# A graph attention stage: 8 of 25 lifts per head made by ScalarE and GpSimd, the rows of maxima read from PSUM by VectorE, and a new order on ScalarE

## The reference, cut to what matters

```python
h = (x @ W).reshape(N, H, C)
al_s = jnp.einsum('nhc,hc->nh', h, a_src)
al_d = jnp.einsum('nhc,hc->nh', h, a_dst)
e = jax.nn.leaky_relu(al_s[src] + al_d[dst], 0.2)
m = jax.ops.segment_max(e, dst, num_segments=N)
ex = jnp.exp(e - m[dst])
denom = jax.ops.segment_sum(ex, dst, num_segments=N)
out = jax.ops.segment_sum(h[src] * (ex / denom[dst])[:, :, None], dst, num_segments=N)
```

## Time and profile before

| | |
|---|---|
| median of the three runs | 4491.51 us |
| the profiled execution's own time | 4485.12 us |
| its span | 4483.3 us |
| VectorE (DVE) busy over the span | 2860.0 us, 64% |
| TensorE (PE) busy | 3600.2 us, 80% |
| ScalarE (ACT) busy | 2241.0 us, 50% |
| GpSimd (POOL) busy | 708.7 us, 16% |
| mean granted TensorE clock | 0.882 of full speed |

### The profile page before, as it was taken

The page is one execution under the profiler, slowest core; times in us unless marked ns, Lnnn a source line. Parts: engine busy times, 40 slices in busy tenths (PEclk is TensorE's granted clock), DMA queues, the critical chain, the costliest instruction groups (busy, mean ns, idle before and its releaser), DMA issues. The chain is left out here.

```text
span 4483.3 us, 70197 instructions
## 1 busy us (share of the span) xinstructions
PE 3600.2 (80%) x21308; PEld 2884.0 (64%) x21309; DVE 2860.0 (64%) x6577; ACT 2241.0 (50%) x5503; POOL 708.7 (16%) x491
## 2 busy tenths in 40 slices
PE   4766999989869999836999999899899268886391
PEld 3333555568768999825777777777778257775160
DVE  6877887811141000239999999999997529996312
ACT  4981367820033444325666666666665457763030
POOL 2991000000023000400111111111110000000404
PEclk9557999999969999958999999999999689996595
DMA  4970234554231111231111111111100323321223
GB/s 121 221 174 13 88 146 177 232 220 147 99 110 45 55 55 55 74 142 35 44 43 43 43 43 43 43 43 43 38 32 39 134 92 107 106 91 39 78 76 107
DMA packets 100401, 396.61 MB, mean 88 GB/s; under 512 B 11870, under 2 KB 56386, under 8 KB 77266
## 3 DMA queue, kind: packets, MB, share of 16 engines
q1 hardware_dynamic: 82940, 344.48, 22.3%
q0 software_dynamic: 14976, 44.58, 3.2%
q10 hardware_dynamic: 2368, 6.03, 0.6%
HBM read 270.45 MB, written 124.59 MB: 88 GB/s over the span
## 5 line engine op out<-in xcount | busy, mean ns | idle before, releaser
L1298 PE MATMUL gat_agg<-f_XN,gat_A 128*128 128x257 f32 x5000 | 1132.8, 385 | 22.1 <-DVE gat_A L1403 22.1
L1298 PEld LDWEIGHTS gat_agg<-f_XN,gat_A 128*128 128x128 f32 x5000 | 956.0, 193 | 163.2 <-DVE gat_A L1403 22.7
L1232 ACT ACTIVATE kept_X<-kept_X,gat_s 128x128 f32<-128x128 f32 x2500 | 741.4, 387 | 481.5 <-DVE kept_X L1392 481.5
L1392 DVE SCALAR_TENSOR_TENSOR kept_X<-gat_r,gat_s 128x128 f32<-128x128 f32 x2500 | 664.9, 345 | 45.8 <-POOL gat_r L1180 45.7
L2312 ACT ACTIVATE moe_exp_h<-moe_exp_hbank,moe_b1c 128x128 f32<-128x128 f32 x742 | 271.3, 367 | 541.1 <-PE moe_exp_hbank L2263 364.8
L868 PE MATMUL mat_cw<-mat_join,mat_lane 128*128 128x400 f16 x2976 | 509.8, 334 | 35.1 <-issue 19.2
L868 PEld LDWEIGHTS mat_cw<-mat_join,mat_lane 128*128 128x128 f16 x2976 | 290.7, 98 | 254.7 <-issue 48.1
L1365 DVE CUSTOM_DVE_ANT_0 gat_junk<-gat_als,gat_absT 128x3200 bf16<-128x3200 f32 x100 | 348.1, 3481 | 25.4 <-DMA gat_als<-score_rows 16.5
L2270 PE MATMUL moe_exp_ybank<-moe_exp_w2b,moe_exp_h 128*128 128x256 f32 x1484 | 350.0, 384 | 9.5 <-DVE kept_X L2332 3.4
L1403 DVE SCALAR_TENSOR_TENSOR gat_A<-kept_X,gat_C 128x1664 f32<-128x1664 f32 x200 | 354.1, 1812 | 0.0
L2346 DVE TENSOR_TENSOR moe_exp_xgT<-moe_exp_ybank,moe_b 128x256 f32 x109 | 46.3, 425 | 460.0 <-PE moe_exp_ybank L2270 460.0
(11 more groups left out here) (369 smaller groups left out, 4699.7 us busy)
## 6 DMA issues: line engine op xcount, KB each, us to landing
gat_C<-count_matrix SPq DMA_DIRECT2D x50, 1600.0 KB, 6.5
count_matrix<-mat_both SPq DMA_DIRECT2D x25, 1600.0 KB, 5.3
weight_matrix<-mat_both SPq DMA_DIRECT2D x25, 1600.0 KB, 8.8
edge_raw<-in_edge_attr_dram SPq DMA_DIRECT2D x50, 768.0 KB, 6.1
e_WT<-weight_matrix SPq DMA_DIRECT2D x13, 1600.0 KB, 6.6
sum_more<-weight_matrix SPq DMA_DIRECT2D x12, 1600.0 KB, 6.6
slot_rows<-moe_exp_xgT POOLq DMA_DIRECT2D x22, 640.0 KB, 3.7
hidden<-gat_h1t SPq DMA_DIRECT2D x25, 512.0 KB, 2.8
```

Of the source, the lines that this page charges most:

```text
L1232: last = nc.scalar.activation(w, w, ACT.Exp, bias=s02[:, t, h:h + 1])
L1298: last = nc.tensor.matmul(agg[h % 2][:, 0:D + 1], A[h % 2][:, t, :], g.XN[:, t, :], start=(t == 0), stop=(t == NT - 1))
L1392: last = nc.vector.scalar_tensor_tensor(out=work[h % 2][:, t * P:(t + 1) * P], in0=r1[:, h, :], scalar=s08[:, t, h:h + 1], in1=r2[:, h, :] ...
```

## The change

In both functions:

- The lift of the last 8 of the 25 tiles of sources (`POOL_TILES`) leaves VectorE. It is written as r2 + max(0.8 d + 0.8 s, 0), which equals max(r1 + s08, r2) since r1 - r2 = 0.8 d. ScalarE makes the positive part (`raise_low`, 8 activations of 128 x 128 into the new buffer `low`), which needs no maximum; GpSimd adds r2 in one instruction of 128 x 1024 (`share`) into `work`. The second half of exps waits for it.
- `rows` moves from GpSimd to VectorE, two instructions per tile, and reads the maxima straight from the PSUM bank. `keep_max` and `m_row` go. `m_diag` goes as well: spread_max multiplies the column m, read as a matrix with equal columns, by the identity (four products of 128 columns in `gat_heads`).
- `low` has one buffer: raise_low of a head waits for the share of the head before it.

In `gat_heads` alone: ScalarE does raise_low of the head after next, then ends, then exps (before: exps, then ends); invert comes before lift; spread_max(i+1) moves to the middle of head 1, behind turn_absent(i+2); rows(i+1) stands in VectorE's list of head 3, ahead of top; the load of `ar` has its own semaphore and waits for raise_low. In `gat_single` alone: rows(i+2) stands between add_output(i-2) and weigh(i), and the bias is added to X at the start, after self_loops(1), not at the end.

```diff
@@ gat_heads: GpSimd
-            def rows(i):
...
+            def share(i, h):
+                n = i * UN + h
+                if h == 0:
+                    wait_alone(pool, r_ready, i * 2 + 2)
+                if not (starts(i) and h < 2):
+                    wait_alone(pool, A_ready, n * 2 - 2)
+                wait_alone(pool, low_ready, n + 1)
+                nc.gpsimd.tensor_tensor(work[h % 2][:, (NT - POOL_TILES) * P:NT * P].rearrange("p (t d) -> p t d", d=P),
+                                        low[:, :].rearrange("p (t d) -> p t d", d=P),
+                                        r2[:, h, :].rearrange("p (o d) -> p o d", o=1).to_broadcast([P, POOL_TILES, P]),
+                                        ALU.add).then_inc(share_ready, 1)
@@ gat_heads: ScalarE
             def exps(i, h):
                 for part, half in enumerate(halves):
                     act.wait_ge(u_ready, (i * UN + h) * 2 + part + 1)
+                    if part == 1:
+                        act.wait_ge(share_ready, i * UN + h + 1)
...
                     ni, nh = following(i, h)
+                    si, sh = following(ni, nh)
+                    if not near_end(si, 0):
+                        raise_low(si, sh)
+                    ends(i, h)
                     if not near_end(ni, 0):
                         exps(ni, nh)
-                    ends(i, h)
                     if h == 1 and not near_end(i, 2):
                         absents(i + 2)
-                    if h == 2 and not near_end(i, 1):
-                        keep_max(i + 1)
...
+            def raise_low(i, h):
+
+                if h == 0:
+                    wait_alone(act, ar_in, i * 16 + 16)
+                if not (starts(i) and h == 0):
+                    wait_alone(act, share_ready, i * UN + h)
+                for t in range(NT - POOL_TILES, NT):
+                    o = t - (NT - POOL_TILES)
+                    last = nc.scalar.activation(low[:, o * P:(o + 1) * P],
+                                                ar[:, at(i % 2), h, :].rearrange("p o d -> p (o d)"), ACT.Relu,
+                                                scale=1.0 - SLOPE1, bias=s08[:, t, h:h + 1])
+                last.then_inc(low_ready, 1)
@@ gat_heads: TensorE
+            def between(i):
+                if not near_end(i, 2):
+                    turn_absent(i + 2)
+                if not near_end(i, 1):
+                    spread_max(i + 1)
+
             def body(i):
                 first = starts(i)
                 for h in range(H1):
-                    head(i, h, first and h < 2,
-                         (lambda: turn_absent(i + 2)) if h == 1 and not near_end(i, 2) else None)
-                    if h == 1 and not near_end(i, 1):
-                        spread_max(i + 1)
+                    head(i, h, first and h < 2, (lambda: between(i)) if h == 1 else None)
@@ gat_heads: VectorE
+            def rows(i):
+
+                mine = ar[:, at(i % 2), :, :].rearrange("p o h d -> p (o h d)")
+                top_row = mrow[:, 0:H1 * P]
+                dve.wait_ge(mrow_ready, i + 1)
+                dve.wait_ge(ar_in, i * 16 + 16)
                 if not starts(i):
...
+                    dve.wait_ge(share_ready, i * UN)
+                    dve.wait_ge(u_ready, i * UN * 2)
+                nc.vector.tensor_tensor(r1[:, :, :].rearrange("p h d -> p (h d)"), mine, top_row,
+                                        ALU.subtract).then_inc(r_ready, 1)
+                nc.vector.scalar_tensor_tensor(out=r2[:, :, :].rearrange("p h d -> p (h d)"), in0=mine, scalar=SLOPE1,
+                                               in1=top_row, op0=ALU.mult, op1=ALU.subtract).then_inc(r_ready, 1)
...
                 for half in halves:
-                    for t in range(half.start, half.stop):
+                    for t in range(half.start, min(half.stop, NT - POOL_TILES)):
...
+                    if h == 3 and not near_end(i, 1):
+                        rows(i + 1)
                     if h == 3 and not near_end(i, 2):
                         top(i + 2, 0)
-                    ni, nh = following(i, h)
-                    if not near_end(ni, 0):
-                        lift(ni, nh)
                     if h >= 2:
                         invert(i, h - 2, starts(i))
                     elif not starts(i):
                         invert(i - 1, H1 + h - 2, False)
+                    ni, nh = following(i, h)
+                    if not near_end(ni, 0):
+                        lift(ni, nh)
@@ gat_single: TensorE
                 if not (isinstance(i, int) and i == 0):
-                    pe.wait_ge(mrow_kept, i)
-                nc.tensor.matmul(mrow[:, 0:P], g.ones[:, :], m_diag[:, :], start=True, stop=True).then_inc(mrow_ready, 1)
+                    pe.wait_ge(r_ready, i * 2)
+                nc.tensor.matmul(mrow[:, 0:P], m[:, 0:1].to_broadcast([P, P]), g.ident[:, :],
+                                 start=True, stop=True).then_inc(mrow_ready, 1)
@@ gat_single: VectorE
                 if not (isinstance(i, int) and i < 2):
                     add_output(i - 2, b)
+                if not near_end(i, 2):
+                    rows(i + 2, b)
                 weigh(i, b)
```

More of the change, by code:

```diff
@@ L1048, in _ @@
             sp.wait_ge(stored, n * 16)
+POOL_TILES = 8
 def gat_heads(nc, sems, g, X):
@@ L1283, in spread_max @@
                 if not starts(i):
-                    pe.wait_ge(mrow_kept, i)
-                nc.tensor.matmul(mrow[:, 0:H1 * P], g.ones[:, :], m_diag[:, :, :].rearrange("p h d -> p (h d)"),
-                                 start=True, stop=True).then_inc(mrow_ready, 1)
+                    pe.wait_ge(r_ready, i * 2)
+                for h in range(H1):
+                    last = nc.tensor.matmul(mrow[:, h * P:(h + 1) * P], m[:, h:h + 1].to_broadcast([P, P]), g.ident[:, :],
+                                            start=True, stop=True)
+                last.then_inc(mrow_ready, 1)
             def head(i, h, early, middle=None):
@@ L1449, in _ @@
             dve.wait_ge(x_out, 16)
+            rows(0)
             lift(0, 0)
@@ L1728, in exps @@
                     act.wait_ge(u_ready, i * 2 + (part + 1))
+                    if part == 1:
+                        act.wait_ge(share_ready, i + 1)
                     for t in range(half.start, half.stop):
@@ L1734, in body, with raise_low @@
             def body(i, b):
+                if not near_end(i, 2):
+                    raise_low(i + 2)
                 if not near_end(i, 1):
                     exps(i + 1, 1 - b)
-                if not near_end(i, 2):
-                    keep_max(i + 2)
                 if not near_end(i, 4):
                     absents(i + 4)
+            def raise_low(i):
+                wait_alone(act, c_in, i * 32 + 32)
+                if not (isinstance(i, int) and i == 0):
+                    wait_alone(act, share_ready, i)
+                for t in range(NT - POOL_TILES, NT):
+                    o = t - (NT - POOL_TILES)
+                    last = nc.scalar.activation(low[:, o * P:(o + 1) * P], ar[:, slot(i), :].rearrange("p o d -> p (o d)"),
+                                                ACT.Relu, scale=1.0 - SLOPE1, bias=s08[:, t:t + 1])
+                last.then_inc(low_ready, 1)
             absents(0)
             absents(1)
-            keep_max(0)
+            act.wait_ge(scaled_s, 1)
+            raise_low(0)
             absents(2)
-            keep_max(1)
             absents(3)
-            act.wait_ge(scaled_s, 1)
             exps(0, 0)
+            raise_low(1)
             tiles(act, body)
@@ L1808, in top @@
                 dve.wait_ge(step, i * PER + 1)
+                if not (isinstance(i, int) and i == 0):
+                    dve.wait_ge(mrow_ready, i)
                 nc.vector.tensor_tensor(m[:, :], mx[:, :], g.AL[:, at(i), 1], ALU.add).then_inc(step, 1)
@@ L1811, in top, with rows @@
                 nc.vector.scalar_tensor_tensor(out=m[:, :], in0=m[:, :], scalar=SLOPE1, in1=m[:, :],
-                                               op0=ALU.mult, op1=ALU.max).then_inc(step, 1)
-                dve.wait_ge(step, i * PER + 3)
-                if not (isinstance(i, int) and i == 0):
-                    dve.wait_ge(mrow_ready, i)
-                nc.vector.tensor_scalar(m_diag[:, :], g.ident[:, :], m[:, 0:1], None, ALU.mult).then_inc(tops_ready, 1)
+                                               op0=ALU.mult, op1=ALU.max).then_inc(tops_ready, 1)
+            def rows(i, b):
+                mine = ar[:, slot(i), :].rearrange("p o d -> p (o d)")
+                dve.wait_ge(mrow_ready, i + 1)
+                if not (isinstance(i, int) and i < 2):
+                    dve.wait_ge(share_ready, i - 1)
+                nc.vector.tensor_tensor(r1[:, b, :], mine, mrow[:, 0:P], ALU.subtract).then_inc(r_ready, 1)
+                nc.vector.scalar_tensor_tensor(out=r2[:, b, :], in0=mine, scalar=SLOPE1, in1=mrow[:, 0:P],
```

(5 more changed lines are left out.)

126 lines of the change are left out of this document (47 added, 79 removed).

## The result

The changed kernel took 4364.85 us (median of four runs, 4360.85 to 4368.09), the kernel before beside it 4491.08 us (four runs, 4490.32 to 4501.12). The ratio is 0.9713, 95% interval 0.9697 to 0.9730: faster by 2.9%. Forecast were 4350 us, with an own range of 4318 to 4372. The time lies in that range, 15 us over the forecast.

The account below looks back on a forecast made before the run. VectorE was taken as the bound, TensorE close behind. `gat_heads` with its earlier first head gave -167 us and `gat_single` +26, together -141: 4350 us in the median's terms, range 4318 to 4372.

Parts of the forecast that it names:

- The stage of four heads: `gat_heads`: TensorE becomes the bound at 50.3 us per tile against 57.0 before; the stage loses 165 us.
- The two unknown prices: `gat_heads`, per tile: two rows instructions from PSUM on VectorE 1.4 us (1.2 to 1.8); eight raise_low activations on ScalarE 2.4.
- GpSimd's addition: `gat_heads`: the 128 x 1024 addition takes 2.5 us and is hidden inside top's 3.48 us.
- the chance that it would overrun: Rival, `gat_heads`: GpSimd's addition takes 8.3 us and keeps VectorE off its lifts; +240 us, about 4757 in all; chance 0.04.
- My threshold of 5.9 us: `gat_heads`: the length of GpSimd's addition from which the kernel turns slower than before.
- ScalarE's new order itself gains nothing while there is this slack: `gat_heads`: putting ends ahead of exps on ScalarE is worth 0 us.
- The ring: `gat_single`: rows before weigh wait for spread_max behind the previous head; 16.6 us per round against 15.1, +33 us.
- three in four: `gat_single`: the share of heads taken to run slowly after TensorE's idle time, 1.4 us more each.
- The upper end of my bounds, +42: `gat_single`: the loss from the ring of waits if the slow clock always counts; +11 if never.
- The bias: End of `gat_single`: its 6.83 us instruction leaves the path, -7 us; at the start it costs 0.
- the 0 to +4 of the forecast: Start of `gat_single`: range for the cost of adding the bias after self_loops(1), taken as 0.
- The load of `ar` behind raise_low: `gat_heads`, SyncE: loads moved past a wait for raise_low cost nothing, covered by a tile of slack.

Follow-up runs that it names:

- e9_lock: The base with GpSimd's share in `gat_heads` also waiting for the first half of the same head's lifts: 4660.49 us (1.0384).
- e5_order: The base with ScalarE's old order in `gat_heads`, exps before ends, raise_low still first: 4435.69 us (0.9889).
- e2_single_before: The base with `gat_single` as before the change and `gat_heads` as changed: 4360.47 us (0.9715).
- The base: The changed kernel with registers loaded from memory clamped from below, outside the attention stages; all experiment kernels stand on it: 4404.39 us (0.9811).

## Why the prediction was right, and where it was wrong

**The stage of four heads was right, for its reasons, and its sum by some luck.** TensorE became the bound at its own pace: a steady tile takes 50.27 us where I had 50.3. The sum, 1262.2 us against 1260.5 (25 x 50.3 and 3), is so near because two misses cancel. The first tile took 60.8 us, 10.5 over the pace, where I had 3 for a slow clock; the last two are 5 us shorter than the pace, since nothing is left to prepare in them and the last is counted to its last product. Most of the 10.5 is a wait that I had not costed, told further down. VectorE was to be busy 47.4 of 50.3 us, 94%, and was at 96%; ScalarE 94%, and was at 92%. The two unknown prices lay within their bounds: rows of 128 x 512 from PSUM 1.3 us for both (2631.72 to 2633.00; 1.4 forecast), eight activations 2.45 (2.4). TensorE waits for nobody in the steady part.

**GpSimd's addition** in the steady part took 2.37 us where I had 2.5, inside top. I had put the chance that it would overrun at 0.04. `e9_lock` shows that the danger was real and its place right: one wait later, the kernel is slower than before. My threshold of 5.9 us cannot be read off that run, since its additions alternate between 3.1 and 6.6.

**"ScalarE's new order itself gains nothing while there is this slack" was wrong.** `e5_order` gives it 31 us. The step that failed was to judge the old order by a slack that I had worked out for the new one. With ends behind exps, and invert ahead of lift as in the change, the steps form a loop of 12.4 us against a head of 11.98; the slack is there because ends comes first. The forecast of the whole did not suffer, since it was summed with the new order in place.

**The ring was right, its size too small.** Its term was 22 x 1.5 = 33 us; measured were 20 rounds of 17.06 against 15.15 before, +38. Three sizes: rows 0.40 and not 0.5, semaphores 0.20 and not 0.1, which cancel, and the slow first half, which I gave to three heads in four, after the four heads that I had looked at. In the 20 rounds all have it: 14.49 in place of the 14.1 that I took. Those heads of before had waited 2.04 us, and over the whole stage of before it was 7 of 11, so my three in four was already high; now TensorE waits 2.4 to 2.6 us in every round, and no round is spared. The upper end of my bounds, +42, was for this.

**The start of `gat_single` was not in the sum at all.** The first round costs 28.7 us and not 15.0 as before: +13.8. I had walked the lists for the steady part and costed the start for VectorE only. The step that I missed is in the diff: raise_low waits for the share of the head before, and on ScalarE exps and absents stand behind it. The last rounds give back 0.9 of the stage's +50.9.

`gat_heads` has the same wait at its start. Its first head came 3.0 us earlier (2.5 forecast), but then ScalarE stood for an addition that weigh had held up, and TensorE for absents:

```profile
2046.69 4.68 POOL L1183 TENSOR_TENSOR kept_X<-gat_low,gat_r 128x1024 f32<-128x1024 f32 x1 [12.96 <-ACT gat_low L1273]
...
2051.47 2.45 ACT L1273 ACTIVATE gat_low<-gat_ar,gat_s 128x128 f32<-128x128 f32 x8 [4.92 <-POOL kept_X L1183]
...
2073.77 2.85 PE L1295 MATMUL gat_absT<-kept_ident,gat_absent 128*128 128x128 bf16 x25 [6.65 <-ACT gat_absent L1226]
```

Head 2 starts 23.2 us after head 1, where a steady tile has 14.3. The first tile of before took 61.0 us, so nothing was lost against before, but nothing was won in it either.

**The bias** left the end (6.83 us, -3.9 measured in the stretch behind the last head, where -7 was forecast), and came back in part at the start, where the stretch between the stages grew by 2.0: inside the 0 to +4 of the forecast. The end gave back 3 us less than the instruction's length. The experiments suggest that this is scatter of that stretch and not a loss: `e2_single_before`, with the bias at the end, has 406.7 us behind its last head, and the eight other experiment kernels, which all have it at the start, have 396.2 to 399.2, so 7.5 to 10.5 less.

**The load of `ar` behind raise_low**, costed at nothing, cost nothing in the changed kernel. Its cover is ScalarE being on time: in `e9_lock`, where it is late, VectorE's rows waited for this load in 6 of 16 tiles, up to 6.3 us.

Together: the span fell by 24 us less than the sum had it, of which the start of `gat_single` is 14, the ring 5 (38 for 33), the two stretches between and behind the stages 5 and the heads of the first stage 2; the last rounds of `gat_single` and the earlier first head gave about 1 back. In the medians 15 us are left of that: I had put the median 6.4 us above the profiled execution, as before, and it came out 3.2 below.

## What to carry to other kernels

When work is moved to free an engine, look for the step with which its list now waits on the next engine directly before what that engine wants: here moving one spread_max from behind a head of 25 products into its middle gave 85 us. Walk the lists once for the steady part and once for the first two rounds, above all where a new buffer is single. And judge an order of steps by the loop that it closes under the new bound, not by the slack that it leaves: here a step that seemed to be worth nothing, by the slack, was worth 31 us.

## What the hardware showed that was not expected

- **GpSimd and VectorE hold each other up in both directions.** The trace of before had only GpSimd standing still. After, at the start of each stage, VectorE does:

```profile
2031.19 6.64 DVE L1425 SCALAR_TENSOR_TENSOR kept_X<-gat_r,gat_s 128x128 f32<-128x128 f32 x17
```

```profile
2031.36 2.38 POOL L1183 TENSOR_TENSOR kept_X<-gat_low,gat_r 128x1024 f32<-128x1024 f32 x1 [126.79 <-DVE gat_r L1415]
```

17 lifts took 6.64 us and not 4.55 while the addition ran at its full 2.38: the second lift stood until the addition was done. The next addition, started at 2046.69 inside weigh's first half, took 4.68 and ended 2.2 us after weigh's second half. The Trainium skill ("SBUF — State Buffer", section on the two separate sides) has it that whichever starts first keeps the ports for its whole instruction. The rows agree where the addition came first: the lift here, and the half of weigh at 2818.93 in `e9_lock`, waited until it was done. They do not fully agree where VectorE came first. The addition came inside weigh's first half and did not get in between the two halves, and in `e9_lock` one came inside the lifts and stood until they and both halves of weigh were done, while at the stages' starts GpSimd did get in between two lifts. What makes the difference was not found.
- **A short idle time of TensorE can cost two thirds as much again.** Each round with about 2.55 us of idle time cost 1.7 us more in the first half of the head, where the granted clock stood at 1.2 GHz and not at 2.4; eight records of useless products (1.89 us) in the gap gave it back.
- **A limit on a register can cost time in a stage of short products.** The base's clamps, one on TensorE's list and one on ScalarE's, made the matrix stage 44 us longer.
